# Routing one chunk earlier, and one block of gathers ahead of a scale, in a macaron block of attention and mixtures of experts

## The chip, the cores and the metric

The kernel is one program on one core of a Trainium2 chip. Its engines are TensorE (PE in the profile), VectorE (DVE), ScalarE (ACT), GpSimd (POOL) and SyncE (SP), which issues most of the DMAs. The metric is the device time of one execution in microseconds (us), less is better. All engines run instruction streams of their own, in order, and meet through semaphores that are waited for explicitly.

## What is computed

Input is x with 4096 rows (tokens) of 256 numbers. Three kinds of layer are applied, each to the layer norm of its input:

```
x = x + 0.5 * ffn0(ln(x))      # 16 experts, 4 chosen, and a shared one
x = x + attn0(ln(x))           # 16 heads, causal, biases
x = x + 0.5 * ffn0(ln(x))
x = x + 0.5 * ffn1(ln(x))      # weights from a table of 16 values
x = x + attn1(ln(x))
x = x + 0.5 * ffn1(ln(x))
```

What matters here of ffn0 is the routing:

```
probs = softmax(xt @ w_router)                 # 4096 x 16
top_w, top_i = top_k(probs, 4); top_w /= sum(top_w)
cw = zeros(T, E).at[rows, top_i].add(top_w)
g = silu(xt @ we1) * (xt @ we3) * cw           # per expert
moe_out = g @ we2
shared = silu(xt @ ws1) * (xt @ ws3) @ ws2
out = shared / 5 + moe_out * 4 / 5
```

Products that need full float32 are made of high and low parts (`_hi`, `_lo`): `hi` is a rounded copy, `lo` the difference, and three matmuls make one product.

## The kernel before, in words

The rows are worked in 8 tiles of 512 (TILES), each of 4 blocks of 128 (SUB). The phases follow each other: routing, experts, projections of attention 0, heads, routing, experts, the table layer, projections, heads, the table layer. The change touches `route_phase` (it runs twice) and, of `project_phase`, only what runs with `combine` set, which is attention 0 alone. The other call of `project_phase` has `combine` empty.

**Routing.** For each tile `t` a loop over 4 chunks `c` (NC = 4) computes the shared expert: TensorE's `gate_up` and, two chunks behind, `down`; ScalarE's gate (Silu, L1781) and `hidden_hi`; VectorE's `product` (L1938, the product of chunk c) and `hidden_lo` (L1943, of the chunk before). In between stands the routing:

- TensorE, by chunk: after `gate_up` and `down`, chunk 0 has `ranks(t)` (it needs the choice of tile t) and the transposes of the first half of the next input, chunk 1 those of the second half (`x_turn`, L1655), chunks 2 and 3 turn back the output of the tile before (`y_turn`, L1712), and chunk 2 has `logits(t+1)` as well. All four kinds of transposes share one buffer, `t_ps`.
- ScalarE: `x_hi` (L1753) copies the turned input in chunks 0 and 1; chunks 2 and 3 split an expert's weights (`split_hi`, L1749); in chunk 3, at the end, `exponent(t+1)` (L1757). Exp and Silu lie in different tables, so each exponent has a table load ahead of it and one behind it.
- VectorE: `x_lo` (L1820) in chunks 0 and 1; `locate(t)` in chunk 1, which turns ranks into row numbers (`rows_at`, L1877); then the moments of tile t+2; `add_y` (L1955) in chunks 2 and 3; `split_lo` (L1967). In chunk 3, behind `split_lo`, `shift(t+1)` (L1826 to L1831, logits less their maximum), `normalise(t+2)` (L1814) and `choose(t+1)` (L1839 to L1856, the four largest of 16, written to `chosen`).
- GpSimd: once `rows_at` of tile t is there, 8 scatters (L1609) of its normalised rows to the experts' regions, the scale `rstd_of(t+2)` (L1601, L1603), and 8 more.
- SP loads two experts' weights, stores and loads a tile of x per step; each load waits for the buffer it overwrites.

**Projections with combine.** Per tile: VectorE adds the experts' rows to x (`combine_rows`, L111), two blocks at a time, takes moments (L559 to L566), GpSimd makes the scale and the shift (`rstd_of`, L338 to L343), ScalarE normalises (L481), TensorE turns the tile (`x_turn`, L379), ScalarE and VectorE split it (`x_hi` L487, `x_lo` L570), TensorE projects. q and k are cut into three bfloat16 parts: ScalarE's `first` and `second`, VectorE's `take_first` and `third`, for m = 0 to 3. TensorE also looks up the weights of a later layer: 16 masks a tile (VectorE, L596) and 48 matmuls (L413), in four quarters; the turned input's buffer is single, and the two halves of the next tile stand before the third and the fourth quarter. The rows that `combine_rows` adds are gathered by GpSimd (L97), 4 gathers a block; a ring of 4 blocks holds them, and a gather waits until the block that it overwrites has been added (`y_used`). GpSimd's order is: all four blocks of tile 0; then for each t a few blocks of tile t+1 (`ahead`: 1 for t = 0, else 2), `rstd_of(t)`, the rest of the blocks.

Of the kernel before, what the change touches and what calls it, by code (L numbers as in the profile page):

```python
# [16 lines left out]
KD = D // P  # L17
TILE = 512
SUB = TILE // P
# [96 lines left out]
def project_phase(nc, name, before, x_in, w_qkv, b_qkv, q_dram, k_dram, v_sb, stack0, first_loaded, consts, combine=None, lookup=None):  # L116
# [7 lines left out]
    with ExitStack() as ctx:  # L124
# [125 lines left out]
        with nc.Block() as block:  # L250
# [80 lines left out]
            @block.gpsimd  # L331
            def _(pool):
                def rstd_of(n):
                    b = n % 2
                    pool.wait_ge(moments_done, n + 1)
                    if n >= 2:
                        pool.wait_ge(xn_ready, n - 1)
                    pool.tensor_tensor(var_eps[:, :], moments[:, :, 1], eps[:, :], ALU.add).then_inc(var_done, 1)  # L338
                    pool.wait_ge(var_done, n + 1)
                    pool.tensor_tensor(rstd[:, b, :], var_eps[:, :], neg_half[:, :], ALU.pow).then_inc(rstd_ready, 1)  # L340
                    pool.wait_ge(rstd_ready, n + 1)
                    pool.wait_ge(minus_ready, n + 1)
                    pool.tensor_tensor(shift[:, b, :], minus[:, :], rstd[:, b, :], ALU.mult).then_inc(shift_ready, 1)  # L343

                def gather(u):
                    gather_rows(pool, u, y_sb, y_used, y_loaded, ys_dram, rows_at)

                pads = v_sb[:, :].rearrange("p (n w) -> p n w", w=VW)
                if combine:
                    for u in range(SUB):  # L350
                        gather(u)
                for t in range(TILES):
                    ahead = 2 if t else 1
                    if combine and t + 1 < TILES:
                        for s in range(ahead):
                            gather((t + 1) * SUB + s)
                    rstd_of(t)
                    if combine and t + 1 < TILES:
                        for s in range(ahead, SUB):
                            gather((t + 1) * SUB + s)  # L360
                pool.memset(pads[:, :, HD:VW], 0.0).then_inc(ones_ready, 1)
                pool.wait_ge(ones_ready, 1)
                pool.memset(pads[:, :, HD], 1.0).then_inc(ones_ready, 1)
                pool.wait_ge(ones_ready, 2)
# [88 lines left out]
            def _(act):  # L453
# [5 lines left out]
                def first(t, m):  # L459
                    act.wait_ge(qk_full, 4 * t + m + 1)  # L460
                    if t >= 2:
                        act.wait_ge(qk_stored[t % 2], 64 * (t // 2))
                    copy_part(parts[:, t % 2, m, part_at(0, m), :], m, qk_ps[:, m, :]).then_inc(first_ready, 1)
# [57 lines left out]
                for t in range(TILES):  # L521
                    if combine and t + 1 < TILES:
                        normalise(t + 1)
                    first(t, 0)
                    first(t, 1)
                    second(t, 0)
                    if not combine and t + 1 < TILES:
                        x_hi(t + 1, 0)
                    first(t, 2)
                    second(t, 1)  # L530
                    if not combine and t + 1 < TILES:
                        x_hi(t + 1, 1)
                    first(t, 3)
                    second(t, 2)
                    second(t, 3)
                    for half in range(2):
                        copy_values(t, half)
                        if not combine and half == 0 and t + 2 < TILES:
                            normalise(t + 2)
                    if not combine:  # L540
                        continue
                    if t + 1 < TILES:
                        for kd in range(KD):
                            x_hi(t + 1, kd)
                    if lookup and t + 2 < PIECES:
                        copy_found(t + 2)

            @block.vector
            def _(dve):
# [49 lines left out]
                def some_masks(t, quarter):  # L599
                    if lookup and t + 2 < PIECES:  # L600
                        masks(t + 2, quarter)
# [49 lines left out]
                for t in range(TILES):  # L651
                    if combine and t + 1 < TILES:
                        combine_rows(t + 1, 0)
                        some_masks(t, 0)
                        some_masks(t, 1)
                        combine_rows(t + 1, 1)
                        find_moments(t + 1)
                    take_first(t, 0)
                    take_first(t, 1)
                    third(t, 0)  # L660
                    if not combine and t + 1 < TILES:
                        x_lo(t + 1, 0)
                    take_first(t, 2)
                    third(t, 1)
                    if not combine and t + 1 < TILES:
                        x_lo(t + 1, 1)
                    take_first(t, 3)
                    third(t, 2)
                    if not combine and t + 2 < TILES:
                        find_moments(t + 2)  # L670
                    some_masks(t, 2)
                    some_masks(t, 3)
                    third(t, 3)
                    if combine and t + 1 < TILES:
                        for kd in range(KD):
                            x_lo(t + 1, kd)

        before.give_way(used)

# [690 lines left out]
def route_phase(nc, name, before, x_in, x_mid, xs_dram, slot_dram, pad_dram, w_router, experts, shared, w_hi, w_lo, rows_at, cw_at, tiles, consts, soft):  # L1370
# [16 lines left out]
    with ExitStack() as ctx:  # L1387
# [147 lines left out]
        with nc.Block() as block:  # L1535
# [210 lines left out]
            def _(act):  # L1746
# [30 lines left out]
                for t in range(TILES):  # L1777
                    for c in range(NC):
                        g = t * NC + c
                        act.wait_ge(g_full, g + 1)  # L1780
                        act.activation(gate[:, g % 2, :], g_ps[:, g % 2, :], ACT.Silu).then_inc(gate_ready, 1)  # L1781
                        if g >= 1:
                            hidden_hi(g - 1)
                        if c < 2 and t + 1 < TILES:
                            x_hi(t + 1, c)
                        if c == 1 and t > 0:
                            copy_y(t - 1)
                        if c >= 2:
                            split_hi(NC + 2 * t + c - 2)
                        if c == 3 and t + 1 < TILES:  # L1790
                            exponent(t + 1)
                hidden_hi(TILES * NC - 1)
                copy_y(TILES - 1)
# [2 lines left out]
            def _(dve):  # L1796
# [186 lines left out]
                for t in range(TILES):  # L1983
                    for c in range(NC):
# [13 lines left out]
                            split_lo(NC + 2 * t - 1)  # L1998
                        if c >= 2 and t > 0:
                            add_y(t - 1, c - 2)  # L2000
                        if c == 3:
                            split_lo(NC + 2 * t)
                        if c == 3 and t + 1 < TILES:
                            shift(t + 1)
                            if t + 2 < TILES:
                                normalise(t + 2)
                            choose(t + 1)
                find_ends()
                hidden_lo(TILES * NC - 1)
                split_lo(NW - 1)  # L2010
# [698 lines left out]
```

## Time and profile before

| | us |
|---|---|
| median of 3 runs | 2897.75 |
| lowest and highest | 2895.61, 2902.35 |
| the profiled execution | 2908.34 |
| its span | 2906.6 |

```profile
span 2906.6 us, 49366 instructions
## 1 busy us (share of the span) xinstructions
PE 2476.0 (85%) x15174; PEld 1604.0 (55%) x15190; DVE 1960.2 (67%) x5524; ACT 1446.0 (50%) x3366; POOL 1095.6 (38%) x1556
## 2 busy tenths in 40 slices
PE   6785998677799999968777994899679999996998
PEclk9887999888889999989988996999788999998999
```

The page gives first each engine's busy time, then the span in 40 slices of 72.7 us: a digit is the busy share in tenths, and PEclk the clock that TensorE was granted, in tenths of full speed. The routings are the slices 1 to 4 and 18 to 21 or so, the projections of attention 0 the slices 8 to 11: there TensorE is at 6 to 8 tenths, elsewhere mostly at 9. PEld is the loading of weights into TensorE.

In the rows further down a timeline row is: start, duration, engine, line, operation, output and inputs, shapes, count of instructions merged; in brackets the idle time of the engine before it and what ended it. "issue" means that nothing in the profile explains the idle time, "remote" that a semaphore moved which no instruction that had just ended explains.

### The profile page before, as it was taken

The page shows a single profiled execution, that of the slowest core. Times are in us where ns is not written, and L with a number is a line of the kernel's source. Part 1 is how long each engine was busy: PE and PEld are TensorE (multiplying, and loading weights), DVE is VectorE, ACT ScalarE, POOL GpSimd, SP SyncE. Part 2 cuts the span into 40 slices and gives each one's busy share as a digit, 9 for nine tenths or more (in the row PEclk, how much of TensorE's full clock was granted, in tenths as well). Part 3 has the DMA queues.
Part 4 walks back from the last instruction along what each step waited for, and adds up shares of the span by engine and source line. Part 5 has one row for each costly group of instructions (what it writes and reads, how often), then busy time and mean ns, then how long its engine had stood idle before and what let it go on. Part 6 is the DMA issues. An engine that isn't in the chain of part 4 may idle for free. (4 is left out here: it accounts for less than half of the span.)

```text
span 2906.6 us, 49366 instructions
## 1 busy us (share of the span) xinstructions
PE 2476.0 (85%) x15174; PEld 1604.0 (55%) x15190; DVE 1960.2 (67%) x5524; ACT 1446.0 (50%) x3366; POOL 1095.6 (38%) x1556
## 2 busy tenths in 40 slices
PE   6785998677799999968777994899679999996998
PEld 5664997344433333347667993677553333334776
DVE  5564887665688878756665884665568887874444
ACT  3332554222358778733334552343456877874443
POOL 4653444766422223316563446662131222230000
PEclk9887999888889999989988996999788999998999
DMA  3434554544634545343435554331373454534000
GB/s 116 151 115 132 179 179 157 176 148 149 163 72 87 116 94 103 95 144 120 149 133 163 178 177 160 91 114 51 127 182 73 82 116 94 103 95 153 30 32 27
DMA packets 251508, 350.78 MB, mean 121 GB/s; under 512 B 42437, under 2 KB 200694, under 8 KB 245110
## 3 DMA queue, kind: packets, MB, share of 16 engines
q1 hardware_dynamic: 212854, 242.71, 32.0%
q0 software_dynamic: 38400, 104.91, 10.1%
q8 instruction: 132, 2.16, 0.4%
q14 instruction: 122, 1.00, 0.1%
HBM read 196.80 MB, written 149.92 MB: 119 GB/s over the span
## 5 line engine op out<-in xcount | busy, mean ns | idle before, releaser
L1299 DVE CUSTOM_DVE_ANT_0 attn_heads_masked_s<-attn_heads_s_ps,attn_heads_causal 128x768 bf16<-128x768 f32 (+7 forms) x1024 | 726.5, 754 | 145.7 <-PE attn_heads_s_ps L1101 130.8
L1218 ACT ACTIVATE attn_heads_probs<-attn_heads_st_ps 128x512 f32<-128x512 f32 (+3 forms) x1536 | 663.1, 494 | 238.2 <-PE attn_heads_st_ps L1120 224.4
L1136 PE MATMUL attn_heads_o_ps<-attn_heads_probs,attn_v_sb 128*32 128x512 f32 (+3 forms) x3072 | 330.4, 503 | 0.2
L1609 POOL DMA_INDIRECT xs_dram<-moe_route_xn,rows_at x256 | 257.2, 1005 | 180.1 <-DVE rows_at L1877 108.2
L1043 POOL TENSOR_SCALAR_AFFINE_SELECT attn_heads_probs<-attn_heads_probs 128x512 f32<-128x512 f32 x256 | 163.3, 638 | 370.0 <-ACT attn_heads_probs L1218 364.9
L1120 PE MATMUL attn_heads_st_ps<-attn_heads_more_st 99*128 99x512 bf16 x960 | 261.6, 329 | 0.1
L1101 PE MATMUL attn_heads_s_ps<-attn_heads_more_st 96*128 96x512 bf16 (+1 forms) x960 | 246.7, 335 | 13.4 <-DMA attn_heads_more_st<-k_dram 8.3
L2105 POOL DMA_DIRECT2D ys_dram<-moe_expert_y_sb x288 | 157.5, 547 | 244.2 <-DVE moe_expert_y_sb L2223 244.1
L1120 PEld LDWEIGHTS attn_heads_st_ps<-attn_heads_more_st 99*128 99x128 bf16 x960 | 84.5, 97 | 213.1 <-ACT attn_heads_probs L1218 157.9
L2137 PE MATMUL moe_expert_gu_ps<-moe_w_hi,moe_expert_xT_hi 128*128 x576 | 189.5, 329 | 1.4 <-DVE moe_expert_xT_lo L2205 1.4
L1101 PE MATMUL attn_heads_s_ps<-attn_stack 96*128 96x512 bf16 (+2 forms) x576 | 157.6, 358 | 26.3 <-DVE attn_heads_row_max L1299 11.3
L97 POOL DMA_INDIRECT attn_stack<-ys_dram,rows_at x128 | 148.3, 1158 | 78.9 <-DVE attn_proj_x_sb L111 36.6
L2179 ACT ACTIVATE moe_expert_xT_hi<-moe_expert_xT_ps 128x256 fp32r<-128x256 f32 x288 | 110.9, 385 | 129.9 <-PE moe_expert_xT_ps L2123 129.3
L2137 PE MATMUL moe_expert_gu_ps<-moe_w_hi,moe_expert_xT_lo 128*128 x576 | 164.0, 285 | 0.0
L2137 PE MATMUL moe_expert_gu_ps<-moe_w_lo,moe_expert_xT_hi 128*128 x576 | 163.7, 284 | 0.0
L97 POOL DMA_INDIRECT lut_y_sb<-ys_dram,rows_at x128 | 133.6, 1043 | 74.1 <-issue 36.1
L1120 PE MATMUL attn_heads_st_ps<-attn_stack 99*128 99x512 bf16 (+3 forms) x576 | 160.3, 337 | 0.9 <-ACT attn_heads_probs L1218 0.7
L413 PE MATMUL attn_proj_w_ps<-attn_proj_mask,attn_proj_diag 128*128 128x512 bf16 x416 | 111.2, 425 | 56.0 <-DVE attn_proj_mask L596 38.6
L2564 DVE SCALAR_TENSOR_TENSOR lut_hid<-lut_gate,lut_u_ps 128x512 f32<-128x512 f32 x80 | 54.9, 686 | 149.9 <-PE lut_u_ps L2397 106.6
L2205 DVE TENSOR_TENSOR moe_expert_xT_lo<-moe_expert_xT_ps,moe_expert_xT_hi 128x256 fp32r<-128x256 f32 x288 | 122.2, 424 | 46.0 <-ACT moe_expert_xT_hi L2179 41.8
L2486 ACT ACTIVATE lut_gate<-lut_g_ps 128x512 f32<-128x512 f32 x96 | 57.2, 596 | 187.1 <-PE lut_g_ps L2397 164.1
L2123 PE MATMUL moe_expert_xT_ps<-ident,moe_expert_x_sb 128*128 128x128 f32 x576 | 113.6, 280 | 34.2 <-DMA moe_expert_x_sb<-xs_dram 32.1
(276 smaller groups left out, 6128.1 us busy)
## 6 DMA issues: line engine op xcount, KB each, us to landing
moe_expert_x_sb<-xs_dram SPq DMA_DIRECT2D x288, 128.0 KB, 2.1
ys_dram<-moe_expert_y_sb POOLq DMA_DIRECT2D x288, 128.0 KB, 2.1
o_dram<-attn_heads_oT SPq DMA_DIRECT2D x64, 256.0 KB, 6.0
moe_route_w_raw<-in_L_ffn_we_dram SPq DMA_DIRECT2D x96, 128.0 KB
q_dram<-attn_proj_parts SPq DMA_DIRECT2D x32, 384.0 KB, 2.8
k_dram<-attn_proj_parts SPq DMA_DIRECT2D x32, 384.0 KB, 2.8
x_mid<-moe_route_x_sb SPq DMA_DIRECT2D x16, 512.0 KB
attn_v_sb<-o_dram SPq DMA_DIRECT2D x32, 256.0 KB
```

The lines of the kernel that those rows point to most:

```text
L97: pool.indirect_dma_start(y_sb[:, r, k, :], None, ys_dram, bass.IndirectOffsetOnAxis(rows_at[:, u, k:k + 1], 0))\
L1043: pool.affine_select(out=d, in_=d, compare_op=ALU.is_ge, fill=0.0, base=0, pattern=[[0, QUAD], [1, P]], channel_multiplier=-1).then_inc(ma ...
L1101: last = pe.matmul(s_ps[:, at + a // TILE, 0:w], q_st(r)[0:DEPTH, h, i * P:(i + 1) * P], k_st(r)[0:DEPTH, h, a:a + w], start=True, stop=True)
L1120: pe.matmul(st_ps[:, v % NB, 0:w], k_st(n % R)[0:ROWS, h, j * P:(j + 1) * P], q_st(n % R)[0:ROWS, h, first:first + w], start=True, stop=Tr ...
L1136: last = pe.matmul(o_ps[h * VW:(h + 1) * VW, use % OB, TILE - w:TILE], v_sb[:, at:at + VW], probs[:, G % NR, h, 0:w], start=(j == 0), stop ...
L1218: act.activation(probs[:, G % NR, h, 0:w], st_ps[:, v % NB, 0:w], ACT.Exp, scale=scale)\
L1299: dve.tensor_tensor_reduce(out=masked_s[:, use % 4, 0:w], in0=s_banks[:, at * TILE:at * TILE + w], in1=causal[:, SEQ - w:SEQ], scale=1.0, ...
L1609: pool.indirect_dma_start(xs_dram, bass.IndirectOffsetOnAxis(rows_at[:, n * SUB + s, k:k + 1], 0), xn[:, n % RX, s, :], None).then_inc(sca ...
L2105: pool.dma_start(ys_dram[s * P:(s + 1) * P, :], y_sb[:, s % AHEAD, :]).then_inc(y_stored[s % AHEAD], 16)
L2123: last = pe.transpose(xT_ps[:, s % 2, kd * P:(kd + 1) * P], x_sb[:, s % AHEAD, kd * P:(kd + 1) * P], ident[:, :])
L2137: last = pe.matmul(gu_ps[:, s % 2, 0:D], a, b, start=(n == 0), stop=(n == len(pairs) - 1))
L2205: dve.tensor_tensor(xT_lo[:, s % RH, :, :].rearrange("p k t -> p (k t)"), xT_ps[:, s % 2, 0:D], xT_hi[:, s % RH, :, :].rearrange("p k t -> ...
```

## The change

In the routing, `logits` stay where they are on TensorE; the work on them moves from chunk 3 to chunk 2: `exponent(t+1)` on ScalarE, `shift(t+1)` and `choose(t+1)` on VectorE, both now one after the other behind `add_y` of chunk 2. In chunk 3 `normalise(t+2)` comes ahead of `split_lo`, with neither `shift` nor `choose` around it. In the projections of attention 0 GpSimd gathers one block ahead of every scale and three behind it. ScalarE splits the first half of the next input (`x_hi(t+1, 0)`) behind `first(t, 3)` and ahead of `second(t, 2)`, `second(t, 3)` and the copies of the values; VectorE does its masks of the third and fourth quarter and `x_lo(t+1, 0)` ahead of `third(t, 2)`. The second halves stay at the end.

```
@@ project_phase, gpsimd
                 for t in range(TILES):
-                    ahead = 2 if t else 1
                     if combine and t + 1 < TILES:
-                        for s in range(ahead):
-                            gather((t + 1) * SUB + s)
+                        gather((t + 1) * SUB)
                     rstd_of(t)
                     if combine and t + 1 < TILES:
-                        for s in range(ahead, SUB):
+                        for s in range(1, SUB):
                             gather((t + 1) * SUB + s)
@@ project_phase, scalar
                     first(t, 3)
+                    if combine and t + 1 < TILES:
+                        x_hi(t + 1, 0)
                     second(t, 2)
                     second(t, 3)
...
                     if t + 1 < TILES:
-                        for kd in range(KD):
-                            x_hi(t + 1, kd)
+                        x_hi(t + 1, 1)
@@ project_phase, vector
                     take_first(t, 3)
+                    some_masks(t, 2)
+                    some_masks(t, 3)
+                    if combine and t + 1 < TILES:
+                        x_lo(t + 1, 0)
                     third(t, 2)
...
-                    some_masks(t, 2)
-                    some_masks(t, 3)
                     third(t, 3)
                     if combine and t + 1 < TILES:
-                        for kd in range(KD):
-                            x_lo(t + 1, kd)
+                        x_lo(t + 1, 1)
@@ route_phase, scalar
-                        if c == 3 and t + 1 < TILES:
+                        if c == 2 and t + 1 < TILES:
                             exponent(t + 1)
@@ route_phase, vector
                             add_y(t - 1, c - 2)
+                        if c == 2 and t + 1 < TILES:
+                            shift(t + 1)
+                            choose(t + 1)
+                        if c == 3 and t + 2 < TILES:
+                            normalise(t + 2)
                         if c == 3:
                             split_lo(NC + 2 * t)
-                        if c == 3 and t + 1 < TILES:
-                            shift(t + 1)
-                            if t + 2 < TILES:
-                                normalise(t + 2)
-                            choose(t + 1)
```

## Rows read from the trace of the kernel before

**Rows 1.** Windows by stretch: length, busy per engine, PEclk, DMA share, GB/s
```profile
0.00:276.00 276.00, 192.96 (x945) 154.60 (x945) 152.52 (x504) 86.46 (x132) 142.48 (x213) 0.87 0.39 129
537.00:767.00 230.00, 171.91 (x793) 105.37 (x805) 129.76 (x363) 71.98 (x142) 142.59 (x133) 0.87 0.46 147
```
**Rows 2.** Line 1877 in both routings: count, ns min/median/max, first and last start
```profile
L1877 DVE TENSOR_SCALAR rows_at<-moe_route_place x8: 174/175/176, 30.3 to 237.1; 128x16 int32<-128x16 f32 x8
...
L1877 DVE TENSOR_SCALAR rows_at<-moe_route_place x8: 174/175/176, 1309.0 to 1508.9; 128x16 int32<-128x16 f32 x8
```
**Rows 3.** Timeline of VectorE, one tile of the first routing
```profile
121.17 0.18 DVE L1877 TENSOR_SCALAR rows_at<-moe_route_place 128x16 int32<-128x16 f32 x1
...
125.40 0.68 DVE L1955 TENSOR_TENSOR moe_route_x_sb<-moe_route_x_sb,moe_route_t_ps 128x512 f32<-128x512 f32 x1
127.41 0.69 DVE L1938 SCALAR_TENSOR_TENSOR moe_route_hid<-moe_route_gate,moe_route_u_ps 128x512 f32<-128x512 f32 x1 [1.33 <-PE moe_route_u_ps L1646]
...
131.65 0.69 DVE L1955 TENSOR_TENSOR moe_route_x_sb<-moe_route_x_sb,moe_route_t_ps 128x512 f32<-128x512 f32 x1 [2.95 <-remote]
...
133.12 0.28 DVE L1826 TENSOR_REDUCE moe_route_logit<-moe_route_r_ps 128x64 f32<-128x128 f32 x1
...
133.84 1.38 DVE L1814 TENSOR_SCALAR moe_route_xn<-moe_route_x_sb,moe_route_moments,moe_route_rstd 128x256 f32<-128x256 f32 x4
```
**Rows 4.** Timeline of ScalarE, the same tile
```profile
127.74 1.28 ACT L1757 ACT_TABLE_LOAD   x1
...
134.23 1.28 ACT L1781 ACT_TABLE_LOAD   x1
135.52 0.60 ACT L1781 ACTIVATE moe_route_gate<-moe_route_g_ps 128x512 f32<-128x512 f32 x1
...
144.75 0.60 ACT L1753 ACTIVATE moe_route_xT_hi<-moe_route_t_ps 128x512 fp32r<-128x512 f32 x1 [8.11 <-remote]
```
**Rows 5.** Timeline of GpSimd, the same tile
```profile
121.62 0.95 POOL L1609 DMA_INDIRECT xs_dram<-moe_route_xn,rows_at  x1 [7.54 <-DVE rows_at L1877]
...
131.75 1.04 POOL L1603 TENSOR_TENSOR moe_route_rstd<-moe_route_var_eps,neg_half 128x4 f32<-128x4 f32 x1
```
**Rows 6.** Timeline of TensorE, the same tile
```profile
131.50 0.39 PE L1646 MATMUL moe_route_y_ps<-moe_route_h_hi,moe_route_s_hi 128*128 128x512 f32 x1
...
137.10 0.18 PE L1646 MATMUL moe_route_r_ps<-moe_route_chosen,moe_route_earlier 128*128 128x16 bf16 x1 [4.04 <-issue]
...
137.48 1.09 PE L1655 MATMUL moe_route_t_ps<-ident,moe_route_xn 128*128 128x128 f32 x4
```
**Rows 7.** Windows: the stretch behind the ranks of the tile before
```profile
108.00:113.30 5.30, 5.30 (x28) 4.43 (x29) 1.45 (x4) 0.00 (x0) 4.08 (x5) 0.50 0.96 326
```
**Rows 8.** Timeline of ScalarE, a tile of the second routing
```profile
1416.68 0.60 ACT L1753 ACTIVATE moe_route_xT_hi<-moe_route_t_ps 128x512 fp32r<-128x512 f32 x1 [3.98 <-PE moe_route_t_ps L1655]
```
**Rows 9.** Line 481, the normalisation, six tiles of the projections
```profile
L481 ACT ACTIVATE attn_proj_xn<-attn_proj_x_sb,attn_proj_shift,attn_proj_rstd x24: 583/584/599, 566.8 to 729.8; 128x256 f32<-128x256 f32 x24
```
**Rows 10.** Timeline of GpSimd, one step of the projections
```profile
648.52 2.56 POOL L97 DMA_INDIRECT attn_stack<-ys_dram,rows_at  x1 [6.86 <-DVE attn_proj_x_sb L111]
...
655.81 0.95 POOL L97 DMA_INDIRECT attn_stack<-ys_dram,rows_at  x1 [0.30 <-issue]
...
661.78 0.22 POOL L338 TENSOR_TENSOR attn_proj_var_eps<-attn_proj_moments,eps 128x4 f32<-128x4 f32 x1
```
**Rows 11.** Timeline of VectorE, the same step
```profile
655.38 0.17 DVE L566 TENSOR_SCALAR attn_proj_minus<-attn_proj_moments 128x4 f32<-128x4 f32 x1
...
671.08 1.81 DVE L596 TENSOR_SCALAR attn_proj_mask<-attn_proj_idx_b 128x512 bf16<-128x512 bf16 x8
```
**Rows 12.** Timeline of ScalarE, the same step
```profile
663.43 2.07 ACT L481 ACTIVATE attn_proj_xn<-attn_proj_x_sb,attn_proj_shift,attn_proj_rstd 128x256 f32<-128x256 f32 x4 [16.08 <-POOL attn_proj_shift L343]
```
**Rows 13.** Timeline of TensorE, the same step
```profile
657.46 5.13 PE L413 MATMUL attn_proj_w_ps<-attn_proj_mask,attn_proj_diag 128*128 128x512 bf16 x23 [0.16 <-issue]
...
676.50 0.60 PE L379 MATMUL attn_proj_t_ps<-ident,attn_proj_xn 128*128 128x128 f32 x4
```

## The prediction

> **What bounds the kernel now.** One core, phases one after the other; the change touches three stretches: the two routing phases and the projections of the first attention. I read first the busy time by stretch [rows 1]. In the first routing TensorE works 193 of 276 us, in the projections 172 of 230, both at a granted clock of 0.87; no engine is near full. So loops of waits set these stretches, and what is won in them goes through to the end, since the phases follow each other.
>
> Routing: the rows of a tile are known (rows_at) eight times per phase, from 30.3 to 237.1 and from 1309.0 to 1508.9 [rows 2]: (237.1 - 30.3)/7 = 29.5 us and 199.9/7 = 28.6 us a tile. I then followed one tile, from rows_at at 121.17 [rows 3]; by the same view its neighbours are at 92.0 and 150.2.
> - GpSimd starts its 16 scatters and a scale at 121.62 after 7.54 idle [rows 5], so 29.1 - 7.5 = 21.6 us is its work, to 143.2. It is the floor of a tile, not its length.
> - VectorE reaches the next logits only at 133.12, behind the addition of 131.65 [rows 3]; the choice follows. TensorE's ranks start at 137.10 after 4.04 idle, and the transposes of the next input are behind them at 137.48 [rows 6]. After such a wait the clock is at its lower level, 1.2 GHz: 0.50 in the stretch behind the ranks of the tile before [rows 7].
> - What is odd: those transposes are over at 138.6, yet ScalarE takes them at 144.75, "remote" [rows 4]. TensorE's semaphore came late, about 1.5 us after the last scatter's issue. In one tile of the second phase the same copy ran at 1416.68 with the transposes as releaser [rows 8], 18.1 us after its rows_at (1398.6 by the view of rows 3), where this tile has 144.75 - 121.17 = 23.6; that tile took 26.1 us, not 29.1. So whether the first half of the input escapes the hold is worth 3 us.
>
> Projections: a step of the loop is (729.8 - 1.5 - 566.8)/5 = 32.3 us: six normalisations of four, the last start less three of them [rows 9]. In the step shown the moments are ready at 655.6 [rows 11], but GpSimd first issues eight gathers (two blocks of 128 rows) and reaches the scale at 661.78 [rows 10]; the normalisation, ScalarE idle 16.08 before it, starts at 663.43 [rows 12]. Behind it stand the parts of q and k, then eight masks at 671.08 [rows 11], then twelve look-up matmuls, then the second transposes at 676.50 [rows 13], which lead to the next step. The moments wait 6 us for their scale, on the path.
>
> **Projections, part by part.** No instruction is added or removed.
> - One block ahead of the scale: the first block's gathers end at 655.81 + 0.95 = 656.8 [rows 10], the moments are there, so the scale runs at 656.8 instead of 661.78: 5.0 us earlier. The other twelve gathers follow it; GpSimd's sum stays 32.3 - 6.9 = 25.4 us [rows 10]. That is the new floor.
> - The first transposes wait for TensorE's look-ups of the first two quarters, which end at 657.46 + 5.13 = 662.6 [rows 13]; the normalisation would end at 660.5, so they run at 662.6.
> - Masks: 5.0 earlier, and 0.7 more since the third part of m = 2 now stands behind them: 665.4. The twelve look-up matmuls end near 668.2 at the upper clock (23 took 5.13, so 12 take 2.7) [rows 13] or near 671 at the lower, which they have now. So the second transposes come at 668.2 to 671 for 676.50: a step of 24.5 to 27.5, with the floor of 25.4. TensorE would idle 2.8 us before the look-ups where it now idles before the first transposes and again before the look-ups, so I lean to the upper clock; but the third and fourth blocks would land just as the additions want them. I take 26.3, 6.0 us a step.
> - Splitting the first half ahead of second(2) costs ScalarE 0.6 us there; TensorE's look-ups cover it, without them it is 0.6 a step.
> - Six scales (tiles 1 to 6) have two blocks ahead of them now. 6 x 6.0 = **36 us**. Bounds: 0 (the blocks land too late, the additions wait as long) to 6 x 6.9 = 41 (the floor). A loss is excluded as long as the second block is there: its gathers end by 656.8 + 1.7 + 5.0 = 663.5, the additions want it after 668.
>
> **Routing, part by part.** The reduction, the maximum, the subtraction and the small steps of the choice move from the fourth chunk to the third; with them the exponent on ScalarE and its two table loads.
> - The addition of the third chunk ends at 126.1 [rows 3]; the logits, ahead of the fourth gate on TensorE, are done (124.1 by the view of rows 6). The shifted logits are ready near 126.9. ScalarE does its first table load at 127.74 to 129.0 already now, idle [rows 4]. Exponent 129.0 to 129.3, choice on VectorE 129.3 to 131.5 after 2.4 us of waiting there. The second load and the gate end at 129.3 + 1.3 + 0.6 = 131.2. product(3), now at 127.41 [rows 3], moves to 131.5.
> - Queued behind it on VectorE are hidden_lo(2), the addition, the normalisation. TensorE wants hidden_lo(2) for down(2) at 131.50 [rows 6] and gets it at 132.8: a new wait of 1.3 us. The ranks, 1.4 behind, find the choice ready: 134.3 for 137.10. So 4.0 idle becomes 1.3.
> - The addition at 132.7 (now 131.65), then the normalisation, no longer behind the logits, 133.4 to 134.8 (now 133.84 to 135.2); GpSimd's scale ends at 131.75 + 1.04 = 132.8, in time [rows 5]. Transposes at 134.9 for 137.48, at the upper clock over at 135.5 for 138.6.
> - That is 14.3 us after rows_at, where the escaped tile copied at 18.1 [rows 8] and this one stood ready at 17.4. I take it that the first half now escapes as a rule: 26.1 us a tile instead of 29.1. Of the twelve steps that follow a full tile two are at 26 already: 10 x 3.0 = 30, and 1 for each of the other four: **34 us**. Bounds: -57 (rival 4) to 14 steps at the 21.6 of GpSimd and 0.7 between, 14 x 6.7 = 94; I take the escaped tile, the nearest row.
> - The low parts of the weights come 1.5 us later on VectorE, and with them SP's loads; three buffers cover that, without them it is 1.5 a tile.
>
> One rule speaks against this. ScalarE's rows show the load of 134.23 done at 135.51 and the gate at 135.52, nothing between [rows 4]. The Trainium skill, "ScalarE: Activation LUTs", section "What ACT_TABLE_LOAD costs", gives 1283 ns and a drain of 1380 ns besides, 2.66 us a switch. By the trace the drain isn't paid here. By the page (estimate) product(3) would be at 134.3, TensorE's new wait 4.1, and the routing would win nothing.
>
> **Sum.** The profiled execution took 2908.3 us (span 2906.6): 2908.3 - 36 - 34 = 2838. The median of the runs, 2897.75, is 10.6 lower; the same difference from it gives **2828**.
>
> **Rivals.**
> 1. The late semaphore is tied to the scatter, not to when the transposes run. For it: in most tiles the copy came 1 to 2 us after the last scatter's issue [rows 4, 5]. Against: rows 8. Routing 0, projections 36: 2862.
> 2. Both halves escape and GpSimd is the bound in both loops: 14 x 6.5 + 6 x 6.9 = 132: 2765. For it: no other engine's work fills a tile. Against: no row shows the second half free of the late semaphore.
> 3. The projections win nothing, because the last blocks land late at a higher load of the queues: 2898 - 34 = 2864. For it: a quarter less time for the same bytes would raise the DMA share of 0.46 [rows 1] to 0.57; against: that is still far from full.
> 4. The other side: the choice in the third chunk holds VectorE, and product(3) pushes the whole tile by its 4.1 us. It decides if hidden_lo(2) comes more than 4 us after TensorE wants it, the idle that it replaces. 14 x 4.1 = 57 slower, less 36: 2919. (The skill's drain would be a way there.)
> 5. It does nothing: the normalisation is hardly earlier, the semaphore is held, and what the gathers give up is waited for elsewhere: 2897.
>
> **Chances.** Forecast 0.40 (2800 to 2848), rival 1 0.22, rival 2 0.13, rival 3 0.10, rival 4 0.08, rival 5 0.07. Faster by over 0.2% (5.8 us, about what a measurement of this kernel can tell from no change): 0.85; same 0.07; slower 0.08. The range 2770 to 2880 holds the forecast, 1 and 3 and part of 2, and leaves out about 0.2.
>
> **What would show it.** Projections: ScalarE idle near 10 and not 16 us before the normalisation, and a step near 26; if the step is 32 with the scale early, the additions wait for a DMA. Routing: TensorE's wait before the ranks gone, one of 1 to 2 us before down(2); the exponent right behind its load; the input's copy 15 us after rows_at, released by the transposes and not "remote"; the clock over 0.9. A copy still 23.6 us after rows_at proves rival 1; a VectorE wait for the exponent over 4 us, rival 4. I am wrong if the tile is still 29 us, or the step 32.

## The result

| where | kernel before, us | changed, us | ratio | 95% interval |
|---|---|---|---|---|
| chip of the forecast (20 runs each) | 2909.98 | 2888.86 | 0.9922 | 0.9907 to 0.9938 |
| chip 13 (e9) | 2907.49 | 2875.24 | 0.9885 | 0.9844 to 0.9925 |
| chip 8 (e18) | 2905.39 | 2870.28 | 0.9888 | 0.9825 to 0.9950 |
| chip 7 (e6) | 2835.81 | 2777.85 | 0.9794 | 0.9768 to 0.9820 |
| chip 0 (e13) | 2836.17 | 2777.43 | 0.9794 | 0.9771 to 0.9817 |

The forecast was 2828 us, 0.976 of its base, in a range of 2770 to 2880. The kernel took 2888.9: faster, but by 0.8% and not by 2.4%, and outside the range. Of the 61 us between, 12 are the base: the three runs that the forecast started from gave 2897.75, twenty give 2909.98. The other rows are from the experiments. The chips fall in two groups, near 2907 and near 2836 us for the same kernel before, and the gain is 21 to 35 us in the one and 58 to 59 in the other.

By the starts of the stages in the two profiled executions on the chip of the forecast (spans 2906.6 and 2889.1, -17.5 us): the first routing gave 10.2 us (its end, the first transposes of the experts' phase, moved from 278.2 to 268.0), the projections 14.3 (from the first q and k matmul to the heads 239.5 us became 225.2), the heads up to the second routing 3.8, the second routing **lost** 9.3 (from its first rows_at to the experts 235.0 became 244.3), and the rest lost 1.5, nearly all of it ahead of the first q and k matmul.

### The profile page after: what moved, and what is told of

It reads as the page before. It is cut to its first block and busy times, and to the rows that moved or that the text cites. A ratio compares the mean times of both kernels' runs of the same rounds, so it can differ in the third digit from the quotient of the medians.

```text
span 2889.1 us, 49366 instructions
## 1 busy us (share of the span) xinstructions
PE 2486.6 (86%) x15174; PEld 1604.9 (56%) x15190; DVE 1963.1 (68%) x5524; ACT 1445.2 (50%) x3366; POOL 1097.0 (38%) x1556
## 3 DMA queue, kind: packets, MB, share of 16 engines
q0 software_dynamic: 38400, 104.91, 10.3%
```

## The profile after, on the chip of the forecast

Windows by stretch, columns as in [rows 1]; the third stretch is the one behind the ranks of a tile, for [rows 7]:

```profile
0.00:276.00 276.00, 199.18 (x983) 157.66 (x984) 155.10 (x514) 89.48 (x142) 146.68 (x214) 0.89 0.41 132
537.00:767.00 230.00, 185.81 (x835) 115.09 (x847) 138.51 (x375) 73.93 (x147) 139.94 (x128) 0.89 0.54 166
...
104.60:107.60 3.00, 2.29 (x10) 1.55 (x11) 0.91 (x2) 1.12 (x2) 2.39 (x3) 1.00 0.77 271
```

The clock behind the ranks is 1.00, full, where it was 0.50: TensorE no longer waits 4 us there. But the tile is no shorter. By the timeline of line 1877 the rows of tiles 2 and 3 are known at 88.49 and 117.58, 29.1 us apart. VectorE, ScalarE and GpSimd in that tile, for [rows 3 to 5]:

```profile
88.49 0.17 DVE L1877 TENSOR_SCALAR rows_at<-moe_route_place 128x16 int32<-128x16 f32 x1
...
94.63 0.29 DVE L1826 TENSOR_REDUCE moe_route_logit<-moe_route_r_ps 128x64 f32<-128x128 f32 x1 [1.23 <-remote]
...
97.23 0.30 DVE L1850 TENSOR_SCALAR moe_route_chosen<-moe_route_top_out 128x64 bf16<-128x64 f32 x1
...
101.15 0.69 DVE L1938 SCALAR_TENSOR_TENSOR moe_route_hid<-moe_route_gate,moe_route_u_ps 128x512 f32<-128x512 f32 x1 [3.04 <-issue]
...
103.22 1.43 DVE L1814 TENSOR_SCALAR moe_route_xn<-moe_route_x_sb,moe_route_moments,moe_route_rstd 128x256 f32<-128x256 f32 x4
```
```profile
95.46 0.26 ACT L1757 ACTIVATE moe_route_top_in<-moe_route_shifted 128x64 f32<-128x64 f32 x1 [4.50 <-DVE moe_route_shifted L1831]
95.74 1.28 ACT L1781 ACT_TABLE_LOAD   x1
97.48 0.60 ACT L1781 ACTIVATE moe_route_gate<-moe_route_g_ps 128x512 f32<-128x512 f32 x1 [0.46 <-remote]
...
104.80 0.60 ACT L1781 ACTIVATE moe_route_gate<-moe_route_g_ps 128x512 f32<-128x512 f32 x1 [5.47 <-remote]
...
112.13 0.60 ACT L1753 ACTIVATE moe_route_xT_hi<-moe_route_t_ps 128x512 fp32r<-128x512 f32 x1 [6.21 <-remote]
```
```profile
88.94 0.95 POOL L1609 DMA_INDIRECT xs_dram<-moe_route_xn,rows_at  x1 [7.07 <-DVE rows_at L1877]
...
109.27 0.96 POOL L1609 DMA_INDIRECT xs_dram<-moe_route_xn,rows_at  x1 [0.30 <-issue]
```

And TensorE, for [rows 6]:

```profile
95.20 0.40 PE L1646 MATMUL moe_route_u_ps<-moe_route_xT_hi,moe_route_s_lo 128*128 128x512 f32 x1
...
102.50 0.50 PE L1646 MATMUL moe_route_y_ps<-moe_route_h_hi,moe_route_s_hi 128*128 128x512 f32 x1 [2.27 <-DVE moe_route_h_lo L1943]
...
104.01 0.18 PE L1646 MATMUL moe_route_r_ps<-moe_route_chosen,moe_route_earlier 128*128 128x16 bf16 x1
...
104.70 0.66 PE L1655 MATMUL moe_route_t_ps<-ident,moe_route_xn 128*128 128x128 f32 x4 [0.18 <-issue]
```

The choice is done at 97.5, 9.0 us after rows_at, as wanted. Three of TensorE's semaphores then come late. The up matmuls end at 95.60, the gate at 98.08, and the product that wants both starts at 101.15 though VectorE was idle; the gate of 104.80 is "remote" for 5.47; the transposes are over at 105.36 and ScalarE copies at 112.13, 23.6 us after rows_at, exactly as before the change [rows 4], 1.9 us after the last scatter's issue. One late semaphore was traded for another: over the whole kernel ScalarE's waits, time in total, times and the longest, were 65.7 us in 10 for the copy and 24.2 in 5 for the gate before, and are now

```profile
ACT moe_route_gate L1781 <- remote: 93.3, 22, 14.3
ACT moe_route_xT_hi L1753 <- remote: 58.9, 9, 7.7
ACT attn_proj_xT_hi L485 <- remote: 39.5, 6, 7.7
```

The last row is new: the projections had no remote wait of their input's copy before. Over all engines the "remote" waits came to 158.0 us in 35 before, and come to 222.4 in 54 now. One step of them, GpSimd, ScalarE and TensorE, for [rows 10, 12, 13]:

```profile
638.60 0.21 POOL L338 TENSOR_TENSOR attn_proj_var_eps<-attn_proj_moments,eps 128x4 f32<-128x4 f32 x1
...
654.70 0.95 POOL L97 DMA_INDIRECT attn_stack<-ys_dram,rows_at  x1 [0.30 <-issue]
```
```profile
640.24 2.07 ACT L479 ACTIVATE attn_proj_xn<-attn_proj_x_sb,attn_proj_shift,attn_proj_rstd 128x256 f32<-128x256 f32 x4 [10.69 <-POOL attn_proj_shift L343]
...
656.05 0.60 ACT L485 ACTIVATE attn_proj_xT_hi<-attn_proj_t_ps 128x512 fp32r<-128x512 f32 x1 [6.93 <-remote]
```
```profile
647.81 5.30 PE L411 MATMUL attn_proj_w_ps<-attn_proj_mask,attn_proj_diag 128*128 128x512 bf16 x12 [3.87 <-DVE attn_proj_mask L595]
652.90 1.05 PE L377 MATMUL attn_proj_t_ps<-ident,attn_proj_xn 128*128 128x128 f32 x4
```

ScalarE idles 10.7 us for 16.1 before the normalisation. The second transposes end at 653.95, but now twelve gathers lie behind the scale and the last is issued at 654.70 to 655.65; the copy comes at 656.05. Before the change the same copy followed its transposes (676.50 + 0.60) at once:

```profile
677.14 0.60 ACT L487 ACTIVATE attn_proj_xT_hi<-attn_proj_t_ps 128x512 fp32r<-128x512 f32 x1 [4.34 <-PE attn_proj_t_ps L379]
```

In the six steps that changed this copy now comes 1.9 to 4.1 us behind the end of its transposes, 17.0 us in all, where it was 0.03 or 0.04 each time. The addition of this step starts at 627.22; the third before it and the third after it (536.14 and 718.24, tiles 1 and 7) stand 182.1 us apart: 30.35 us a step. Before the change it was (743.23 - 545.06)/6 = 33.03. Counted by the normalisations as the forecast did, 32.3 became (700.39 - 554.32)/5 = 29.2.

## The experiments

The theory: the change does what the forecast's steps say, but on some chips TensorE's semaphores come late while GpSimd's indirect DMAs are in flight, and take it back. The rival: the steps themselves are worth less. In each diff "-" is the kernel that it starts from.

**e1 to e4, the parts alone (chip 6, before 2834.17).** The kernel before with the routing's edits alone (e1), the projections' alone (e2), of these the gather order alone (e3) or the split and the masks alone (e4):

```
e3, GpSimd:   - ahead = 2 if t else 1        + ahead = 1
e4, ScalarE:  + x_hi(t + 1, 0)  (ahead of second(2))
    VectorE:  some_masks(t, 2), (t, 3) and x_lo(t + 1, 0) ahead of the last third part
```

> Only the routing's part of the change; the projections are as before. Theory H (TensorE's semaphores are held back while scatters are in flight, whenever the transposes run): a tile stays near 29 us, the copy of the turned input still about 23 us after rows_at and 'remote', and of the change's 22 us the routing has at most 8: ratio to before 0.997 to 1.001. The forecast's theory (the copy escapes because it is ready earlier): 34 us, ratio 0.988.

> Only the projections' part; the routing is as before. Theory H: the six steps go from 32.5 to 29.5 or 30 us, 16 to 20 us in all, ratio 0.993 to 0.995, so that this part is nearly the whole change. The forecast's size (6.0 us a step): 36 us, ratio 0.988.

> Only GpSimd's order in the projections: one block of gathers ahead of each scale; ScalarE and VectorE split both halves of the next input at the end, as before. If the scale's place is the whole gain (forecast): the normalisation starts 5 us earlier in each step, and 14 to 18 us are won, ratio 0.994 to 0.995; the split adds 0.7 us a step, 4 us, at most. If the split is needed for it: under 5 us, ratio above 0.998.

> Only the split of the next input amid the parts, with the masks ahead of third(2); GpSimd gathers two blocks ahead of each scale as before. Forecast: masks 0.7 us earlier, so about 0.7 us a step, 4 us, ratio 0.998 to 0.999. Rival: the copy of the first half waits on ScalarE for TensorE ahead of second(2), and the step gets longer: ratio 1.001 or more.

Measured: e1 2806.21 us, 0.9914 (0.9891 to 0.9937); e2 2805.17, 0.9901 (0.9880 to 0.9922); e3 2799.22, 0.9891 (0.9870 to 0.9911); e4 2832.85, 0.9994 (0.9978 to 1.0009). No row of these traces is "remote". So each part earns 28 to 29 us where semaphores are in time. The projections' part is the gather order, which alone earns 35 (its interval overlaps that of e2), and the split earns nothing there. In e1 a tile takes 22.45 us (105.09, 127.54, 150.00): GpSimd waits for nothing in it, its issues follow each other 0.3 us apart.

**e5 and e6, both kernels as they are (chip 7, before 2835.81).**

> The kernel before, unchanged, for its trace on the chip of the experiments. Theory C (the late semaphores of TensorE belong to the chip or its state, not to the kernel): on a chip where it runs in 2834 us no wait ends 'remote', a routing tile takes about 24 us and a projection step 32.5; where it runs in 2900, they are there and the tile takes 29. Theory H (the kernel's scatters always hold the semaphores back): 29 us and 'remote' everywhere.

> The changed kernel, unchanged. Theory C: without the late semaphores the forecast's mechanism works in both parts: projection step near 26.5, routing tile 22.4 (GpSimd's work without a pause), ratio 0.980 to 0.985, the two parts' ratios (0.9914 and 0.9901) nearly multiplied. Rival: the parts overlap or the measured 0.9922 holds on every chip: ratio 0.990 to 0.994.

Measured: 2835.78, 0.9998 (0.9979 to 1.0017), and 2777.85, 0.9794 (0.9768 to 0.9820). Line 1877, then ScalarE and TensorE in one tile of the changed kernel, whose rows_at is at 104.53:

```profile
L1877 DVE TENSOR_SCALAR rows_at<-moe_route_place x16: 174/175/177, 31.0 to 1385.6; 128x16 int32<-128x16 f32 x16
...
110.46 1.28 ACT L1781 ACT_TABLE_LOAD   x1
111.76 0.60 ACT L1781 ACTIVATE moe_route_gate<-moe_route_g_ps 128x512 f32<-128x512 f32 x1
...
119.46 0.66 PE L1655 MATMUL moe_route_t_ps<-ident,moe_route_xn 128*128 128x128 f32 x4 [1.55 <-DVE moe_route_xn L1814]
...
120.15 0.60 ACT L1753 ACTIVATE moe_route_xT_hi<-moe_route_t_ps 128x512 fp32r<-128x512 f32 x1 [4.24 <-PE moe_route_t_ps L1655]
```

The copy starts 0.03 us behind the transposes. Between the first and the last rows_at of a phase lie 160.2 us, 22.9 a tile; in e5 it is (207.97 - 30.91)/7 = 25.3 and 24.8. The stages from e5 to e6: routings -16.2 and -13.1, projections -31.1 (a step 33.0, then (660.54 - 495.80)/6 = 27.5; by the normalisations 32.3, then 26.7, where the forecast had 26.3), the rest +0.7: -59.7. The table load and the gate stand 0.02 us apart. The Trainium skill ("ScalarE: Activation LUTs", section "What ACT_TABLE_LOAD costs") has 1380 ns of drain on top of a load's 1283. The trace does not agree, here without late semaphores nor in [rows 4] with them.

**e7, four scatters more per tile (chip 7), from the changed kernel.**

```
- SCATTERED = SUB * TOP_K * 16
+ SCATTERED = (SUB + 1) * TOP_K * 16
+ for k in range(TOP_K):
+     pool.indirect_dma_start(xs_more, bass.IndirectOffsetOnAxis(rows_at[:, t * SUB, k:k + 1], 0), xn[:, t % RX, 0, :], None)...
```

> The changed kernel with 4 more scatters at the end of each routing tile, into an array that nobody reads (5.1 us more of GpSimd's work a tile). Theory G (in the change the scatters bound a routing tile when no semaphore is late): each tile 5.1 us longer, 14 x 5.1 + 2 x 5.1 = 80 us slower than the changed kernel. On a chip with late semaphores, theory H: the copy of the turned input moves with the scatter's end, also by 5 us. Rival: another chain bounds the tile and hides the extra scatters: under 30 us.

Measured: 2850.69, 1.0056 (1.0034 to 1.0077), 72.8 us more than e6. Sixteen tiles by four times 1.26 (issue 0.96, gap 0.30) are 80.6: GpSimd's issues bind the tile there, which is the forecast's rival 2.

**e8, the next input's second transposes ahead of the third quarter of the look-ups (chip 7).**

```
- some_lookup(t, 2)
  (x_turn(t + 1, 1))
+ some_lookup(t, 2)
```

> The changed kernel, with TensorE turning the second half of the next input ahead of the look-ups of the third quarter, not behind them. The twelve look-ups (2.7 to 5.3 us) leave the path: the second transposes come behind x_lo(t+1, 0), at most 3 us earlier. If the projection step is bound by that path: 6 x 2 to 3 us less than the changed kernel, 12 to 18 us. If GpSimd's gathers (25.4 us a step) bound it already: at most 6 x 1.1 = 6 us.

Measured: 2779.46, 0.9797 (0.9769 to 0.9824): e6 again. A step takes 26.5 for 27.5, and the projections 204.6 us for 208.7. But nothing of it is left in the whole: the heads up to the second routing took 527.1 for 520.6, and why was not followed up.

**e9 to e12 (chip 13, before 2907.49): a chip of the other group.** e9 and e18 are the changed kernel; e10 changes the gather order in the dense layer behind the second routing (L2384); e11 is the changed kernel without the split; e12 adds a wait to GpSimd.

```
e10, dense layer:  - ahead = 2 if t else 1    + ahead = 1
e11:               x_hi, x_lo and some_masks where they were before
e12, ahead of scatter(t, range(2, SUB)):  + pool.wait_ge(t_free, TURN["x", t + 1, 0] + 1)
```

> The changed kernel as it is, once more. Theory (the gain hangs on whether TensorE's semaphores come late beside the indirect scatters): where the copy of the first input half starts within 0.1 us of its transposes and no wait is 'remote', a routing tile takes 22.5 us and the ratio to the kernel before is 0.979 (0.977 to 0.982); where that copy is 'remote' 23 us after rows_at, a tile takes 29 us, the kernel before some 2900 us, and the ratio is 0.992. Rival (the two ratios are drift between measurements and nothing of the chip): a ratio between the two, whatever the waits show.

> The changed kernel, and in the first dense layer after the second routing (same GpSimd loop: gathers of the next tile, then the scale) one block ahead of the scale and not two. Theory (the reorder pays only where the moments wait for their scale on the path, and there TensorE already works 152 of 167 us): 0 to 6 us less, ratio to the changed kernel 0.998 to 1.000. Rival (the reorder pays 5 us in any loop with eight gathers ahead of the scale): 6 steps of 5 us, 30 us less, ratio 0.989.

> The changed kernel without its edits of the split: routing as changed, one gather block ahead of the scale, but the split of the next input and the masks where they were before. Theory (the split alone gave 0.9994, the gathers alone more than both together, so it is worth nothing): within 0.2% of the changed kernel, step of the projections near 27. Rival (it earns what the forecast gave it, 0.6 to 1.3 us a step, once the gathers have moved): 4 to 8 us slower than the changed kernel.

> The changed kernel, with one wait more on GpSimd in the routing: the second eight scatters of a tile (tiles 1 to 6) start only when the first half of the next input has been copied out of PSUM. Theory (semaphores come late only beside scatters in flight, and otherwise the tile is bound by GpSimd): without 'remote' waits the second eight start at 15.8 us after rows_at and not at 13.6, so a tile takes 24.5 to 25.1 for 22.5 and the run is 25 to 31 us slower than the changed kernel; with them, the copy escapes and a tile takes 26 for 29, some 30 us faster. Rival (the late semaphore has nothing to do with scatters in flight, or the scatters are not the bound): on a chip with 'remote' waits the tile stays 29 us or more; on one without, the time stays.

e9: 2875.24, 0.9885. Copies of the input come 23.6 us after rows_at in the trace (87.72 and 111.28). How many tiles escape differs from one execution to the next: of the 14 steps between rows_at 1 is under 27 us in the profiled execution of the forecast's chip (span 2889.1), 2 in e9 (2878.2), 3 in e18 (2870.8). e12 below, in which the added wait held nothing, has 3 (2871.3). Such a tile is worth 3 to 5 us, so it can explain a part of the spread of 2867 to 2902 in the table's first row, not all of it.

e10: **2906.83**, 1.0006 (0.9984 to 1.0027), 31.6 us slower than e9: both theories had it at or below the changed kernel. From the layer's first transposes to those of the second attention, 255.5 us became 287.3. ScalarE's waits in that layer, e10:

```profile
ACT lut_gate L2486 <- PE lut_g_ps L2397: 101.5, 39, 5.5
...
ACT lut_xT_hi L2481 <- DMA attn_heads_sums<-o_dram: 19.5, 5, 4.5
ACT lut_xT_hi L2481 <- PE lut_t_ps L2406: 8.5, 6, 2.1
ACT lut_xT_hi L2481 <- issue: 8.2, 4, 2.1
```

The DMA named has nothing to do with this layer; it is a semaphore that no record explains. e9 has 71.5 us in the first row, nothing in the second, 7.6 and 2.6 in the last two. With one block ahead of the scale more gathers lie behind it, where the input is turned and copied. In the same stretch TensorE's clock fell from 0.98 to 0.91. That the late copies cause the loss is argued from these rows, not shown.

e11: 2888.68, 0.9945 (0.9922 to 0.9969), 13.4 us slower than e9, against both theories. Not clean: its projections took 234.7 us, 222.8 in e9 but 231.3 in e18, and its second routing, whose code is that of e9, took 11.1 more (247.8 for 236.7). Its profiled execution was also the slowest of its ten (2902.8, median 2888.7). What the split is worth on such a chip stays open.

e12: 2875.51, 0.9895 (0.9858 to 0.9932), as e9. The wait named an input that had long been copied; GpSimd did not wait for it, and so the run says nothing on either theory.

**e13 to e15 (chip 0, before 2836.17), the gap as meant.** e14 and e15 are the changed kernel with

```
e14  + if 0 < t < TILES - 2: pool.wait_ge(t_free, TURN["x", t + 2, 0] + 1)
e15  + if 0 < t < TILES - 2: pool.wait_ge(t_free, TURN["x", t + 2, 1] + 1)
```

> The changed kernel, for the comparison on the same chip. Theory: ratio 0.988 to 0.992 where the kernel before takes some 2900 us (late semaphores), 0.979 where it takes some 2835.

> The changed kernel with one wait more on GpSimd: the second eight scatters of tile t (t = 1 to 5) start only when the first half of input t+2 has been copied out of PSUM, about 15 us after rows_at. (In the run before, the wait named input t+1, which had long been copied, so it opened no gap.) Theory (semaphores come late only beside scatters in flight; without them the tile is bound by GpSimd): on a chip with late semaphores the first copy comes right behind its transposes, 15 to 16 us after rows_at and not 23.6, and the tile takes 26 to 27 us for 29: 20 to 30 us faster than the changed kernel. On a chip without, the second eight start 2.6 us later and it is 10 x 2.6 = 26 us slower. Rival (the late semaphore comes when it comes, whatever GpSimd does): the copy stays at 23 us after rows_at, with the second scatters behind it, and the tile takes 33 us or more: 40 us slower or worse.

> As the run before, but the second eight scatters wait for the second half of the input too, about 20 us after rows_at. Theory: on a chip with late semaphores both halves escape, but the last scatter's issue ends at 20 + 10 = 30 us after rows_at: a tile of 30 us, 10 us slower in all than the changed kernel; on one without, 5 x 2 tiles at 30 for 22.5, 75 us slower. Rival: on a chip with late semaphores far slower, 35 us a tile.

Measured: e13 2777.43, 0.9794; e14 2817.08, 0.9937 (0.9915 to 0.9959), +39.7; e15 2862.57, 1.0084 (1.0062 to 1.0106), +85.1. Without late semaphores GpSimd binds, and what it is held back is lost (26 and 75 had been expected). In e14's trace the gap is 4.4 us in each of the ten tiles, where 2.6 had been expected.

**e16 to e18 (chip 8, before 2905.39): the gap where semaphores come late.** e16 is the kernel of e14, e17 that of e10, e18 the changed kernel.

> The gap of the run before last once more (second eight scatters of a tile behind the copy of the first input half), for a chip with late semaphores. Theory (late only beside scatters in flight): there the copy comes 15 to 16 us after rows_at and a tile takes 26 to 27 us for 29, 20 to 30 us faster than the changed kernel. Rival (late whatever GpSimd does): copy at 23 us, a tile of 33 us, 40 us slower or worse. On a chip without late semaphores 40 us slower than the changed kernel (ratio 0.994), as measured before.

> The gather order in the dense layer again. On the chip with late semaphores it was 1.1% slower than the changed kernel, with 19 us of late copies of the input where there were none. Theory (that loss is the late semaphores' alone): on a chip without them 0 to 6 us faster than the changed kernel, ratio to the kernel before 0.977 to 0.980; on one with them 1.0. Rival (the order itself costs in a loop that TensorE bounds): 10 us slower or more on any chip.

> The changed kernel, for the comparison on the same chip: 0.979 without late semaphores, 0.988 to 0.992 with them.

e16: 2910.75, 1.0027 (1.0003 to 1.0051), 40.5 us slower than e18. One tile of it, rows_at at 114.81; GpSimd, VectorE, TensorE and ScalarE in this order:

```profile
129.13 0.96 POOL L1609 DMA_INDIRECT xs_dram<-moe_route_xn,rows_at  x1 [0.30 <-issue]
...
140.54 1.49 POOL L1609 DMA_INDIRECT xs_dram<-moe_route_xn,rows_at  x1 [9.09 <-DVE moe_route_xT_lo L1822]
...
126.98 0.29 DVE L1828 TENSOR_REDUCE moe_route_logit<-moe_route_r_ps 128x64 f32<-128x128 f32 x1 [7.25 <-remote]
...
137.80 1.09 PE L1657 MATMUL moe_route_t_ps<-ident,moe_route_xn 128*128 128x128 f32 x4
...
132.66 0.60 ACT L1783 ACTIVATE moe_route_gate<-moe_route_g_ps 128x512 f32<-128x512 f32 x1 [3.28 <-remote]
...
138.93 0.60 ACT L1755 ACTIVATE moe_route_xT_hi<-moe_route_t_ps 128x512 fp32r<-128x512 f32 x1 [3.42 <-PE moe_route_t_ps L1657]
```

In the gap the copy comes 0.04 us behind the transposes (137.80 + 1.09), and so in 10 of the 10 tiles that have a gap; in e18, without gaps, this copy is 2.2 to 7.1 us late in tiles 1 to 5 of the first routing. In eight of the ten the transposes themselves run only some 24 us after rows_at, when the scatters would be over anyway. The two that decide are tile 1 of each routing: there the copy comes 14.8 and 15.9 us after rows_at, in time, and in e18 it is 5.8 and 6.0 us late. The first of them, rows_at at 61.45:

```profile
76.20 0.60 ACT L1755 ACTIVATE moe_route_xT_hi<-moe_route_t_ps 128x512 fp32r<-128x512 f32 x1 [1.53 <-PE moe_route_t_ps L1657]
```

So the late semaphore goes with the scatters in flight: that part of the theory is shown. DMA traffic as such is not enough for it. In the experts' phase (330 to 480 us of the changed kernel on the forecast's chip) the DMA share is 0.55 with 178 GB/s; in a tile's scatters (121 to 143 of the kernel before) it is 0.49 with 174. Yet in the experts' phase no wait is "remote". But the hold moved to the first eight scatters: the logits, on the path of the choice, are "remote" for 7.25 us until 126.98, and the gate of 132.66 comes 12.2 us behind its matmuls. The normalisation comes behind them, the tile takes 31.0 us (114.81, 145.76), and neither the 26 to 27 of the theory nor the 33 of the rival was measured. The whole, 40 us slower, is what the rival had, though not by its mechanism. Of the 31.9 us between the two traces 20.6 lie where there is no gap: from the rows_at of tile 6 to that of tile 7 it is 39.9 and 39.7 us, for 28.6 and 30.4 in e18.

e17: 2909.33, 1.0004 (0.9971 to 1.0037), 39 us slower than e18. Its copies wait 17.8 us under the same wrong name and another 10.3 under "issue". The time of e10 is repeated. What this order does in the dense layer without late semaphores wasn't measured.

## Why the prediction was wrong

- **"I take it that the first half now escapes as a rule: 26.1 us a tile".** This step failed. The forecast took an escape for a matter of when the transposes run. It is a matter of what is in flight: scatters lie over 21.6 of a tile's 29.1 us, and transposes 16 us after rows_at fall inside them, at 14.3 as well. On the forecast's chip 34 us were to come of the routing; the first gave 10.2, of which 2.0 are the start of its first tile, the second lost 9.3. Rival 1 (p 0.22) named it. What the forecast read as a copy free of the hold [rows 8] was not: its transposes end 1.3 us before it, where a copy in time comes 0.04 us behind, and in the other short tile it was 2.0 us late and "remote". Which tiles are short changes from one trace to the next, and the changed kernel had one in that trace for two before. In the steps between rows_at the first routing gained 3.5 us and the second lost 8.9; 4.7 of the first's gain lie behind its last rows_at. The 2.0 of the start are no part of the gain: e4, whose routing is that of before, starts at 28.2 as well.
- **The steps up to there were right.** Wait before the ranks gone; new wait before down 2.27 us, for 1.3; clock full behind the ranks. The exponent came 7.0 us after rows_at, for 7.8, though not right behind its load: its table was there early and it waited 4.50 us for the shifted logits. Where semaphores are in time, the two routings gave 29.3 us for 34: a tile of 22.5 in the steady part, by rival 2's bound and not by an escape, from 25 and not from 29.
- **Projections, 36 us: the scale 5 us earlier was right, the step of 26.3 was not, on this chip.** It waits 1.2 us for GpSimd (637.37 to 638.60) and not 6. Measured were 6 x 2.7 = 16 us by the additions, 14.3 by the stages. What took the rest is the second half's copy: it is 17.0 us late over the six steps, 2.8 a step, and the step is 2.9 longer than on chip 7. The reorder has put twelve gathers behind the scale, over the transposes; before, the last gather's issue was over at 673.5 and the second half was turned at 676.50. The forecast costed the moved gathers as time on GpSimd and as late data, and not as company for TensorE's semaphores. Where these are in time the step went from 33.0 to 27.5 and the stage gave 31.1.
- **The clock in the look-ups**, leaned to the upper level: in the step shown it was the lower (5.30 us for 12, where 11 took 2.78 behind them). This was part of the term's range.
- **The range** reached to rival 1 and its 2862, with the projections whole in it. That rival and the loss of half of the projections are one mechanism, so they come together: 2898 - 16 is 2882, by the same base. The forecast had the row for it (the copy 1.5 us after the last scatter's issue, [rows 4, 5]) but applied it to the routing alone.
- **Two slips that decide nothing.** Rival 3 has "a quarter less time", but 32.3 to 26.3 is a fifth; its 0.57 is right for that, and 0.54 was measured. And GpSimd's sum in the step of [rows 10] is 25.0 us, not 25.4: that step is 33.0 long.

## What to carry to other kernels

Where one row of the profile is unexplained ("remote", or a wait for a DMA of another layer), find out what is in flight in every place where it shows before costing a change that moves other work into such a stretch; here a reorder worth 5.5 us a step gave 2.7, and the same edit in a loop bounded by TensorE cost 32 to 39 us on such chips, for a reason that was not shown. Price a mechanism once for all stages, not as a rival in one of them. And measure on more than one chip: a loop whose waits hang on such semaphores gained 0.8% on one and 2.1% on another.

## What was not expected of the hardware

- The same kernel takes 2905 to 2910 us on the chip of the forecast and on chips 13 and 8, and 2834 to 2836 on three others, at clocks of 0.919 and 0.926. On the slower ones TensorE's semaphores come late while GpSimd's indirect DMAs are in flight: the input's copy up to 8 us behind the end of its transposes, the gate up to 12.8 in the changed kernel (224.18). Every "remote" wait of these traces ends beside an indirect DMA's issue or at most 3.9 us behind it; on the others no wait is "remote". TensorE itself also pauses there: in the routings of the kernel before it has 11 idle times over 1 us that nothing explains, 50.2 us in all, for 2 and 8.1 us in e5.
- With the gap of e16 the copy's semaphore takes 0.04 us, and the logits' one, beside the scatters, 8. Why these chips differ, and by what way the scatters hold the semaphores, no run shows.
- GpSimd's indirect DMA takes 0.95 us and 0.30 between two, in some rows 2.56 to 2.86 [rows 10].
